# Unrolled middle batches, and softmax row shifts turned from columns to rows through DRAM

## The chip, the cores and the metric

One core of a Trainium2 chip runs the whole program. The metric is the device time of one execution in microseconds (us), as the median of the runs; the profile is of one further execution, and its own time is given beside it. The engines are named as in the profile: PE (matmul, with PEld for its weight loads), DVE (vector), ACT (scalar), POOL (GpSimd) and SP (the queue that issues nearly all DMAs).

## What is computed

A decoder layer on 16 batches of 256 tokens of width 128: a gated recurrence, cross-attention over 1601 context rows per batch with 16 heads of 64, and a mixture of 8 feed-forward experts, each followed by a layer norm. Nearly all of the time goes to the cross-attention:

```python
q = (x @ Wq + bq).reshape(b, lq, H, D)
k = (embeds @ Wk + bk).reshape(b, lk, H, D)
v = (embeds @ Wv + bv).reshape(b, lk, H, D)
scores = jnp.einsum('bqhd,bkhd->bhqk', q, k) * SCALE
attn = jax.nn.softmax(scores, axis=-1)
ctx = jnp.einsum('bhqk,bkhd->bqhd', attn, v).reshape(b, lq, AD)
return ctx @ Wo + bo
```

## The kernel before

The attention works through 16 batches times 8 pairs of heads. One pair of one batch is called a slot here; there are 128. Scores are made with the keys on the partitions and the 256 queries along the free axis, in 7 score units of up to two key tiles for both heads. So the softmax's row maximum, which is subtracted before the exponential, has to stand along the free axis too. It is found one slot ahead: for slot s + 1, PE makes the scores a second time with the queries on the partitions (`maximum`, L1304), DVE takes their maxima (`maxima`, L991), and `row_shift` on DVE reduces them to a negated column `nm` for each of the two query tiles (L998, first and second tile; the second comes after `keys_low` of chunk 0). The column is then widened to 128 equal columns (`nspread`, L1003), PE transposes both tiles (L1312) into a PSUM bank, and ACT copies the bank to `shift` (L742). The first of four matmuls of each score tile adds `shift` (L1330).

A slot runs in this order. PE: maxima of slot s + 1 and score units of slot s in turn; then values (L1293 to L1295) and keys (L1277 to L1279) of later slots, queries (L1284), in the second slot of a batch the output projection (L1360), the two transposes (L1312), in the sixth slot the transposes of the next batch's context (L1266), the denominators of slot s - 1 (L1351), and the product of slot s with the values (`attend`, L1342). ACT: `heads_out` (copy of the previous slot's product to `heads_raw`, L752), 14 exponentials (L763, L766), copies of values (L736), keys (L720) and queries (L725), `shift_out` (L742), in the sixth slot four copies of context (L716), and `sums_out` (copy of the denominators to `den`, L747). DVE: 16 maxima, `row_shift`, the low parts of keys and queries (L978, L984), in the sixth slot those of the context (L972), in the second `finish_rows`, and last `reciprocals` (L1009) and `normalise` (L1018), which makes `heads_T` from `heads_raw` and `rden`.

`heads_out` of a slot waits until the `normalise` of the slot before has read `heads_raw`:

```python
def heads_out(at, r):
    wait(act, norm_ok, at.n(1, r, 0))
    act.wait_ge(ring_full, at.full("pv", r))
    copy(heads_raw[:, :], ps[:, at.place_of("pv", r), 0:T]).then_inc(ring_act, 1)
```

The 8 PSUM banks go round as a ring in the order that `batch_fills` writes out: each product takes the bank that the product eight places before it has left. Of a slot's last products, `den` and `pv` hold the banks that score unit 1 of the next slot takes.

Each engine keeps its own order. The first and the last batch are written out (`batch(Batch("first", 0, B))` and so on); the 14 batches between are one body in a loop (`Fori`) on PE, ACT, DVE and POOL. SP has a loop of its own that loads the next batch's context once its place is read, and is otherwise idle during the attention. Every wait is a semaphore wait of the engine at the head of its queue: what stands behind it waits too.

## Time and profile before

| | us |
|---|---|
| median of 3 runs | 3018.2 |
| lowest and highest run | 3013.98 and 3557.24 |
| the profiled execution | 3013.75 |
| its span | 3011.9 |
| PE busy | 2779.7 (92%) |
| DVE busy | 2175.8 (72%) |
| POOL busy | 2125.0 (71%) |
| ACT busy | 1689.3 (56%) |

The span is the time from the first to the last instruction of the profiled execution. Rows of a timeline give the start in us from the start of the span, the duration in us, and then engine, source line, operation, the tiles written and read, and the count of merged instructions; what stands in brackets is idle time before the row and what ended it. A matmul's end is modelled; the distance between starts is the firmer number.

### The profile page before, as it was taken

The numbers are of one execution on the slowest core, as the hardware profiler recorded it, in microseconds if no ns is written. First come the engines' busy times: TensorE is split into PE (matmuls) and PEld (weight loads), VectorE is DVE, ScalarE is ACT, GpSimd is POOL, SyncE is SP. The second block draws the span as 40 slices with busy tenths as digits, with TensorE's granted clock in tenths as the row PEclk, the third lists the DMA queues.
The fourth block names the chain that finished last, engine by engine and source line by source line (L and its number), as shares of the span: only waits on it lengthen the run. The fifth ranks groups of instructions, "written<-read, shape, count | busy, mean of one in ns | idle before, by whom it ended". The sixth has DMA issues, their size and how long they took to land.

```text
span 3011.9 us, 80484 instructions
## 1 busy us (share of the span) xinstructions
PE 2779.7 (92%) x28504; PEld 2321.9 (77%) x28504; DVE 2175.8 (72%) x4113; ACT 1689.3 (56%) x3422; POOL 2125.0 (71%) x1708
## 2 busy tenths in 40 slices
PE   5799999999999999999999999999999999997371
PEld 3688888888888888888888888888888888886250
DVE  6777877877777778778777778778787777784104
ACT  2466665656656656656566666556566666663020
POOL 2377877777777777777777777777787777786305
PEclk8799999999999999999999999999999999998586
DMA  3100000000000000000000000000000000000032
GB/s 95 44 2 13 2 13 3 13 3 13 3 2 14 2 14 2 13 2 13 3 13 3 2 13 2 14 2 13 3 13 3 27 3 2 2 2 1 23 92 63
DMA packets 65430, 41.89 MB, mean 14 GB/s; under 512 B 6614, under 2 KB 62635, under 8 KB 65010
## 3 DMA queue, kind: packets, MB, share of 16 engines
q1 hardware_dynamic: 62962, 32.35, 3.8%
q8 instruction: 266, 4.36, 0.6%
q0 software_dynamic: 2048, 3.91, 0.5%
q14 instruction: 154, 1.26, 0.1%
HBM read 28.15 MB, written 8.39 MB: 12 GB/s over the span
## 4 chain that ended last, share of the span: by engine, by line
PE 89%; issue 5%; POOL 3%; DVE 1%; ACT 1%; DMA 0%; POOLq 0%; DVEq 0%; ACTq 0%
PE ps L1330 28%; PE ps L1342 24%; PE ps L1304 7%; PE ps L1293 4%; PE ps L1294 3%; PE ps L1295 3%; PE ps L1277 3%; PE ps L1278 3%; PE ps L1279 3%; PE ps L1351 2%; PE ps L1360 2%; PE ps L1284 2%; PE ps L1450 1%; PE ps L1457 1%; PE ps L1312 1%
## 5 line engine op out<-in xcount | busy, mean ns | idle before, releaser
L600 POOL TENSOR_TENSOR key_sums<-key_sums,prob_T 128x512 f32<-128x512 f32 (+1 forms) x1408 | 1812.3, 1287 | 124.3 <-ACT prob_T L763 8.1
L991 DVE TENSOR_REDUCE mx<-ps 128x1 f32<-128x400 f32 (+1 forms) x2048 | 1070.0, 570 | 476.4 <-PE ps L1304 438.9
L763 ACT ACTIVATE prob_T<-ps 128x512 f32<-128x512 f32 x1536 | 834.3, 596 | 222.0 <-PE ps L1330 203.3
L1342 PE MATMUL ps<-prob_T,v_sb 128*64 128x256 f32 (+1 forms) x6656 | 742.3, 380 | 0.8 <-ACT prob_T L766 0.8
L1342 PEld LDWEIGHTS ps<-prob_T,v_sb 128*64 128x64 f32 (+1 forms) x6656 | 478.4, 137 | 243.3 <-issue 2.1
L596 POOL TENSOR_TENSOR key_sums<-prob_T 128x512 f32<-128x512 f32 x128 | 165.1, 1290 | 509.8 <-ACT prob_T L763 509.8
L1330 PE MATMUL ps<-shift,shift_w 64*128 64x256 f32 (+1 forms) x3328 | 507.3, 300 | 0.3 <-DVE k_lo L978 0.2
L1330 PE MATMUL ps<-q_lo,k_hi 64*128 64x256 f32 (+1 forms) x3328 | 476.0, 279 | 1.8 <-issue 1.8
L1330 PE MATMUL ps<-q_hi,k_lo 64*128 64x256 f32 (+1 forms) x3328 | 474.1, 279 | 0.0
L1330 PE MATMUL ps<-q_hi,k_hi 64*128 64x256 f32 (+1 forms) x3328 | 473.0, 279 | 0.0
L752 ACT COPY heads_raw<-ps 128x256 f32<-128x256 f32 x128 | 47.7, 373 | 671.9 <-PE ps L1342 671.9
L1304 PE MATMUL ps<-k_hi,q_hi 64*128 64x400 f32 (+1 forms) x2048 | 371.2, 357 | 26.4 <-issue 23.4
L978 DVE SCALAR_TENSOR_TENSOR k_lo<-ps,bk_c,k_hi 128x400 fp32r<-128x400 f32 (+1 forms) x512 | 309.9, 625 | 57.1 <-ACT k_hi L720 51.9
L1330 PEld LDWEIGHTS ps<-shift,shift_w 64*128 64x128 f32 (+1 forms) x3328 | 310.2, 181 | 52.7 <-ACT prob_T L763 8.2
L1330 PEld LDWEIGHTS ps<-q_lo,k_hi 64*128 64x128 f32 (+1 forms) x3328 | 314.3, 183 | 3.2 <-issue 3.2
L1330 PEld LDWEIGHTS ps<-q_hi,k_lo 64*128 64x128 f32 (+1 forms) x3328 | 312.5, 182 | 0.0
L1330 PEld LDWEIGHTS ps<-q_hi,k_hi 64*128 64x128 f32 (+1 forms) x3328 | 312.4, 183 | 0.1
L720 ACT ACTIVATE k_hi<-ps,bk_c 128x400 fp32r<-128x400 f32 (+1 forms) x512 | 302.8, 596 | 13.1 <-PE ps L1279 9.8
L1304 PEld LDWEIGHTS ps<-k_hi,q_hi 64*128 64x128 f32 x2048 | 195.9, 186 | 77.6 <-issue 76.8
L736 ACT COPY v_sb<-ps 128x512 f32<-128x512 f32 x384 | 225.7, 588 | 52.9 <-PE ps L1295 25.8
L1293 PE MATMUL ps<-wv_hi,ctx_hi 128*128 128x256 f32 (+1 forms) x832 | 246.9, 297 | 0.0
L1009 DVE RECIPROCAL rden<-den 128x256 f32<-128x256 f32 x128 | 223.9, 1749 | 25.2 <-ACT den L747 24.8
(173 smaller groups left out, 3641.9 us busy)
## 6 DMA issues: line engine op xcount, KB each, us to landing
ctx_raw<-in_ctx_dram SPq DMA_DIRECT2D x16, 768.0 KB
tables<-in_L_ffn_W_dram SPq DMA_DIRECT2D x16, 256.0 KB, 3.9
slots_in<-zeros SPq DMA_DIRECT2D x32, 64.0 KB
xs<-in_x_dram SPq DMA_DIRECT2D x8, 256.0 KB, 3.2
xres<-in_x_dram SPq DMA_DIRECT2D x8, 256.0 KB, 2.9
v_sb<-slots_in SPq DMA_DIRECT2D x8, 256.0 KB, 2.8
slots_out<-v_sb SPq DMA_DIRECT2D x8, 256.0 KB, 4.1
out_dram<-x1s SPq DMA_DIRECT2D x8, 256.0 KB, 2.4
```

Source lines behind the costliest of these rows:

```text
L596: op = nc.gpsimd.tensor_tensor(acc[:, :, :], prob_T[:, :, 0, :], prob_T[:, :, 1, :], ALU.add)
L600: op = nc.gpsimd.tensor_tensor(acc[0:rows, :, :], acc[0:rows, :, :], prob_T[0:rows, :, k, :], ALU.add)
L720: nc.scalar.activation(k_hi[r % 2][:, KEY0[c]:KEY0[c] + WID[c]], ps[:, at.bank("k", r, c), 0:WID[c]], ACT.Identity, bias=bk_c[:, r % NJ:r ...
L736: copy(v_sb[:, g % 2, 2 * n:2 * n + 2, :], src).then_inc(ring_act, 1)
L763: nc.scalar.activation(prob_T[:, h, 2 * i:2 * i + 2, :].rearrange("p k t -> p (k t)"), ps[:, bank, :], ACT.Exp).then_inc(ring_act, 1)
L978: v.scalar_tensor_tensor(k_lo[r % 2][:, cols], ps[:, at.bank("k", r, c), 0:WID[c]], bk_c[:, r % NJ:r % NJ + 1], k_hi[r % 2][:, cols].bitca ...
L991: v.tensor_reduce(mx[:, qt, h, c:c + 1], ps[:, at.bank("mx", r, c, qt, h), 0:WID[c]], AX.X, ALU.max).then_inc(ring_dve, 1)
L1009: v.reciprocal(rden[:, :], den[:, :]).then_inc(rden_ok, 1)
L1293: mm(o, ctx_hi[:, cols], wv_hi[:, g0:g0 + 2 * P], start=True, stop=False)
L1304: mm(ps[:, banks[h], 0:WID[c]], q_hi[r % 2][lanes, qt * P:qt * P + P], k_hi[r % 2][lanes, KEY0[c]:KEY0[c] + WID[c]], start=True, stop=True ...
L1330: last = mm(ps[0:rows, banks[h], n * T:n * T + T], keys_part, query_part[lanes, :], start=(step == 0), stop=(step == 3))
L1342: last = mm(ps[h * DH:h * DH + DH, bank, 0:T], v_sb[0:rows, r % NJ // 2 % 2, k, v0 + h * DH:v0 + h * DH + DH], prob_T[0:rows, h, k, :], st ...
```

## The change

Two things are done at once. The 14 middle batches are written out on PE, ACT, DVE and POOL instead of looped over, and SP's instructions for them too. And the column `nm` is no longer widened and transposed by PE: SP stores it to DRAM, word by word, as rows, waits for that store, and reads it back twice, once for each head, each time as one 1 KB row broadcast to 64 partitions of a new tile `shift_f`; ACT rounds `shift_f` to `shift`. The bank `sh` of the ring, the copies L1003 and the transposes L1312 fall away.

```diff
@@ batch_fills
-        put("act", "sh", 0)
...
-        if following:
-            put("act", "sh", s + 1)
@@ decoder_layer
+    shift_dram = nc.dram_tensor("row_shifts", [2, 2 * QT, P], F32, kind="Internal").ap()
...
-        nm = sb("nm", [P, QT, 2])
-        nspread = sb("nspread", [P, QT, P])
+        nm = sb("nm", [P, 2, QT])
+        shift_f = sb("shift_f", [P, T])
@@ SP
+            def turn_shift(at, r):
+
+                sp.wait_ge(nm_ok, at.n(2, r, 2))
+                if at.kind != "start" and (at.kind != "first" or r > 1):
+
+                    sp.wait_ge(shift_in, at.n(32, r, -32))
+                with nc.allow_non_contiguous_dma(reason="a column of 128 values for each head and tile"):
+                    sp.dma_start(shift_dram[r % 2].rearrange("n p -> p n"), nm[:, :, :].rearrange("p h q -> p (h q)"))\
+                        .then_inc(shift_sent, 16)
+                sp.wait_ge(shift_sent, at.n(16, r, 16))
+                wait(sp, shift_ok, at.n(1, r, 0))
+                for h in range(2):
+                    sp.dma_start(shift_f[h * DH:h * DH + DH, :],
+                                 shift_dram[r % 2, h * QT:h * QT + QT, :].rearrange("q p -> (q p)")[None, :].broadcast_to([DH, T])).then_inc(shift_in, 16)
+
+            def batch(at):
+                for s in range(NJ):
+                    if s < NJ - 1 or at.kind != "last":
+                        turn_shift(at, s + 1)
+                    if s == 5 and at.kind != "last":
+                        next_context(at)
+
+            def next_context(at):
+
+                sp.wait_ge(ctx_hi_ok, at.b * 4 + 8)
+                load_context(at.b + 2)
+
             load_context(0)
-            with sp.Fori(1, B) as b:
-
-                sp.wait_ge(ctx_hi_ok, b * 4)
-                load_context(b)
+            sp.wait_ge(ctx_hi_ok, 4)
+            load_context(1)
+            turn_shift(Batch("start", 0, B), 0)
+            batch(Batch("first", 0, B))
+            for b in range(1, B - 2):
+                batch(Batch("mid", b, B))
...
@@ POOL; ACT, DVE and PE alike
-            with pool.Fori(1, B - 1) as b:
+            for b in range(1, B - 1):
                 batch(Batch("mid", b, B))
@@ ACT
             def shift_out(at, r):
-                act.wait_ge(ring_full, at.full("sh", r))
-                copy(shift[:, :], ps[:, at.bank("sh", r), 0:T]).then_inc(ring_act, 1)
+                act.wait_ge(shift_in, at.n(32, r, 32))
+                copy(shift[:, :], shift_f[:, :]).then_inc(shift_ok, 1)
@@ DVE
             def maxima(at, r, units):
+
+                wait(dve, nm_ok, at.n(2, r, 0))
...
-                v.tensor_reduce(nm[:, qt, :], mx[:, qt, :, :], AX.X, ALU.max, negate=True).then_inc(nm_ok, 1)
-                dve.wait_ge(nm_ok, at.n(2, r, qt + 1))
                 if qt == 0 and at.kind != "start" and (at.kind != "first" or r > 0):
 
-                    dve.wait_ge(ring_full, at.full("sh", r - 1))
-                v.tensor_copy(nspread[:, qt, :].rearrange("p (h d) -> p h d", h=2),
-                              nm[:, qt, :, None].broadcast_to([P, 2, DH])).then_inc(nspread_ok, 1)
+                    dve.wait_ge(shift_sent, at.n(16, r, 0))
+                v.tensor_reduce(nm[:, :, qt], mx[:, qt, :, :], AX.X, ALU.max, negate=True).then_inc(nm_ok, 1)
@@ PE
-            def row_shift(at, r):
-
-                pe.wait_ge(nspread_ok, at.n(2, r, 2))
-                bank = bank_of(at, "sh", r)
-                for qt in range(QT):
-                    last = tr(ps[:, bank, qt * P:qt * P + P], nspread[:, qt, :], ident[:, :])
-                last.then_inc(ring_full, 1)
-
             def score_unit(at, s, i):
...
-                                 also=[("k", s, 3), ("q", s), ("sh", s)] if i == 0 else [])
+                                 also=[("k", s, 3), ("q", s)] if i == 0 else [])
+                if i == 0:
+                    pe.wait_ge(shift_ok, at.n(1, s, 1))
```

## Rows read from the trace of the kernel before

**Rows 1.** The page: busy time and share of each engine
```profile
PE 2779.7 (92%) x28504; PEld 2321.9 (77%) x28504; DVE 2175.8 (72%) x4113; ACT 1689.3 (56%) x3422; POOL 2125.0 (71%) x1708
```
**Rows 2.** Windows cut at slots' first exponentials: from:to, length, busy time by engine, PEclk
```profile
300.37:2611.77 2311.40, 2286.10 (x24322) 1932.41 (x24321) 1790.30 (x3207) 1429.59 (x2912) 1767.97 (x1400) 1.00 0.03 7
2611.77:2632.20 20.43, 20.43 (x220) 17.09 (x218) 16.42 (x27) 13.00 (x26) 15.39 (x12) 1.00 0.01 2
2632.20:2655.15 22.95, 22.95 (x243) 19.62 (x241) 17.61 (x37) 12.25 (x26) 18.07 (x16) 1.00 0.01 1
...
199.54:218.92 19.38, 19.38 (x211) 16.00 (x209) 15.49 (x28) 12.13 (x26) 15.46 (x12) 1.00 0.01 2
239.29:260.04 20.75, 20.75 (x224) 17.47 (x222) 17.79 (x32) 13.62 (x30) 15.48 (x12) 1.00 0.15 41
179.16:199.54 20.38, 20.38 (x220) 17.05 (x218) 16.21 (x28) 13.01 (x27) 15.42 (x12) 1.00 0.01 2
```
**Rows 3.** Waits of PE: engine, line, releaser: total us, times, longest us
```profile
PE ps L1304 <- issue: 23.4, 13, 2.1
```
**Rows 4.** Timeline of PE, batch 0, third slot
```profile
191.51 0.38 PE L1312 MATMUL ps<-ident,nspread 128*128 128x128 f32 x2
191.82 0.65 PE L1351 MATMUL ps<-key_sums,ones 128*64 128x256 f32 x4
```
**Rows 5.** Groups by line: busy us, mean ns of one, idle before
```profile
L1003 DVE COPY nspread<-nm 128x128 f32<-128x128 f32 x256 | 222.9, 871 | 18.7
```
**Rows 6.** Timeline of ACT, batch 0, third slot and start of the fourth
```profile
192.13 0.37 ACT L742 CAST shift<-ps 128x256 fp32r<-128x256 f32 x1
192.58 0.37 ACT L747 COPY den<-ps 128x256 f32<-128x256 f32 x1
198.19 0.37 ACT L752 COPY heads_raw<-ps 128x256 f32<-128x256 f32 x1 [5.24 <-PE ps L1342]
199.54 1.71 ACT L763 ACTIVATE prob_T<-ps 128x512 f32<-128x512 f32 x3 [0.97 <-PE ps L1330]
```
**Rows 7.** Timeline of DVE, the same slot
```profile
192.98 1.75 DVE L1009 RECIPROCAL rden<-den 128x256 f32<-128x256 f32 x1
194.77 1.16 DVE L1018 TENSOR_TENSOR heads_T<-heads_raw,rden 128x256 f32<-128x256 f32 x1
```
**Rows 8.** The tile heads_T: durations in ns, shortest, median and longest
```profile
L1018 DVE TENSOR_TENSOR heads_T<-heads_raw,rden x128: 424/802/1505, 174.4 to 2777.4; 128x256 f32<-128x256 f32 x128
```
**Rows 9.** Timeline of DVE, batch 0, sixth slot
```profile
248.88 0.15 DVE L998 TENSOR_REDUCE nm<-mx 128x2 f32<-128x8 f32 x1
...
252.33 2.01 DVE L972 TENSOR_TENSOR ctx_lo<-ps,ctx_hi 128x512 fp32r<-128x512 f32 x4
```
**Rows 10.** Timeline of ACT, the same slot
```profile
251.27 0.37 ACT L742 CAST shift<-ps 128x256 fp32r<-128x256 f32 x1
251.52 1.70 ACT L716 CAST ctx_hi<-ps 128x512 fp32r<-128x512 f32 x4
```
**Rows 11.** Timeline of SP's queue, the same slot: start and duration of an issue
```profile
253.44 0.40 SPq L505 DMA_DIRECT2D ctx_raw<-in_ctx_dram  x1
254.06 0.52 SPq L507 DMA_DIRECT2D ctx_raw<-in_ctx_dram  x1
```
**Rows 12.** DMA issues: KB each, median us from issue to landing
```profile
slots_out<-v_sb SPq DMA_DIRECT2D x8, 256.0 KB, 4.1
...
w_rows<-in_L_attn_Wr_dram SPq DMA_DIRECT2D x1, 64.0 KB, 1.9
...
bo_b<-in_L_xattn_bo_dram SPq DMA_DIRECT2D x1, 64.0 KB, 2.7
decay_c<-in_L_attn_decay_dram SPq DMA_DIRECT2D x1, 0.5 KB, 2.1
...
bq_c<-in_L_xattn_bq_dram SPq DMA_DIRECT2D x1, 4.0 KB, 7.0
...
bv_c<-in_L_xattn_bv_dram SPq DMA_DIRECT2D x1, 4.0 KB, 3.4
```
**Rows 13.** Timeline of DVE, before the first slot
```profile
136.49 0.16 DVE L998 TENSOR_REDUCE nm<-mx 128x2 f32<-128x8 f32 x1
```
**Rows 14.** Timeline of PE, first score tile of the first slot
```profile
138.68 0.39 PE L1330 MATMUL ps<-shift,shift_w 64*128 64x256 f32 x2 [0.19 <-DVE k_lo L978]
```

More of the change, by code:

```diff
@@ L420, in decoder_layer @@
         nm_ok = sem("nm_ok")
-        nspread_ok = sem("nspread_ok")
+        shift_sent = sem("shift_sent")
+        shift_in = sem("shift_in")
+        shift_ok = sem("shift_ok")
         rden_ok = sem("rden_ok")
@@ L510, in load_context @@
                              C_IN[bass.ds(b * KEYS + KEYS - 1, 1)]).then_inc(ctx_in, 16)
-            load_context(0)
-            with sp.Fori(1, B) as b:
-                sp.wait_ge(ctx_hi_ok, b * 4)
-                load_context(b)
+            def turn_shift(at, r):
[19 more added lines that the diff above has]
+                load_context(at.b + 2)
+            load_context(0)
+            sp.wait_ge(ctx_hi_ok, 4)
[4 more added lines that the diff above has]
+                batch(Batch("mid", b, B))
+            at = Batch("mid", B - 2, B)
+            for s in range(NJ):
+                turn_shift(at, s + 1)
+            batch(Batch("last", B - 1, B))
             def load_weights(i, s):
@@ L807, in _ @@
             batch(Batch("first", 0, B))
-            with act.Fori(1, B - 1) as b:
+            for b in range(1, B - 1):
                 batch(Batch("mid", b, B))
@@ L1081, in _ @@
             batch(Batch("first", 0, B))
-            with dve.Fori(1, B - 1) as b:
+            for b in range(1, B - 1):
                 batch(Batch("mid", b, B))
@@ L1384, in batch @@
                         project(at)
-                    if following:
-                        row_shift(at, s + 1)
                     if s == 5 and more:
@@ L1407, in _ @@
             queries(at, 1)
-            row_shift(at, 0)
             batch(Batch("first", 0, B))
-            with pe.Fori(1, B - 1) as b:
+            for b in range(1, B - 1):
                 batch(Batch("mid", b, B))
```

## The prediction

> **What bounds the kernel now.** First the page's busy times [rows 1]: PE is busy for 92% of the span, DVE and POOL for 72% and 71%, ACT for 56%. An average hides stages, so next I cut the attention at the first exponential of each slot [rows 2]. The 14 looped batches take 2311.40 us, 165.1 each, with PE busy for 2286.10 of it; inside a slot PE has no idle time at all. So what comes off PE's queue shortens the slot, as long as nothing else becomes late. The waits of PE show where its 25 us of idle go: 13 times it stood still for 1.8 us on average (23.4 us in all), waiting for no one, ahead of the first maximum of a batch [rows 3]. Thirteen is the number of times that the loop goes back from the end of one of the 14 batches to the start of the next.
>
> **The loops.** Batch 0 and batch 15 are written out already, so they show what a written-out slot takes [rows 2]: 20.43 us for the first slot of a batch, 22.95 for the second, 20.38 for the third (the fifth and seventh do the same work, three in all), 19.38 for the fourth (the eighth does the same, two in all, with one value tile group fewer than the third), 20.75 for the sixth with the context. The sum is 20.43 + 22.95 + 3 x 20.38 + 2 x 19.38 + 20.75 = 164.03 us. Against 165.1 that is 1.07 us a batch, 15 us for 14. The stalls are worth 23 us, but the written-out slots are each a little slower than looped ones, or the difference would be larger. I take -15 (bounds 0, if new code stalls elsewhere, and -23).
>
> **PE's transposes.** Start to start, the two transposes take 191.82 - 191.51 = 0.31 us [rows 4], on the bounding engine, in each of 128 slots: -39.7 us. The matmul added in their place is none; a wait on `shift_ok` replaces one on the ring.
>
> **DVE's copies.** 256 copies of 871 ns, 222.9 us [rows 5], fall away. They cost nothing today: `row_shift` ends microseconds before PE needs it and DVE is idle each slot. I count 0. What they do is move the second `nm` forward. In the sixth slot the first copy happened to be short, and `nm` ended at 248.88 + 0.15 = 249.03, 9.74 us after the slot's start at 239.29 [rows 2, 9]. I use 9.74 for every slot after the change. ACT's copy stays, with SBUF instead of PSUM as its source, at 0.37.
>
> **The way through DRAM.** Call T the time from the end of the second `nm` to the start of ACT's copy. Its terms:
> - SP wakes: 0.2. ACT's last `ctx_hi` ends at 251.52 + 1.70 = 253.22 and SP issues at 253.44 [rows 10, 11].
> - The store, 128 partitions of 4 single words. No row shows a store of words. Nearest are loads of words [rows 12]: 128 words land after 2.1 us (`decay_c`), 1024 words after 3.4 (`bv_c`), and after 7.0 where 512 KB loads are ahead of them (`bq_c`). By interpolation 512 words take 2.1 + 384/896 x 1.3 = 2.7. Bounds 2.1 and 7.0. I take 2.7: with SP otherwise idle nothing is ahead, and the store of 65536 words in rows of 512 B lands after 4.1, so direction alone is not dear.
> - SP wakes again, 0.2, and issues the first load; the second follows 254.06 - 253.44 = 0.6 later [rows 11].
> - Each load is 64 KB. 64 KB land after 1.9 us (`w_rows`) or, as a broadcast row behind the bias loads, 2.7 (`bo_b`) [rows 12]. I take 2.0, and 0.1 for ACT to wake.
>
> T = 0.2 + 2.7 + 0.2 + 0.6 + 2.0 + 0.1 = 5.8 us; bounds 5.1 and 10.8.
>
> On the page "DMA: Bandwidth & Descriptors" (Anatomy of one DMA) the Trainium skill gives about 2.0 us fixed for each small transfer, most of it the receipt of the write. By it the store would take 2.0 and T would be 5.1, the low bound of the rows, which gives the 2962 us of the first rival below instead of 2977. The figure is fitted on GpSimd's path, and `decay_c` (2.1) agrees with it.
>
> **Who waits.** PE's next scores are not the first to suffer. ACT now waits for the loads at the head of its queue, and `sums_out` is behind it; DVE's reciprocal and `normalise` wait for `den`; and the next `heads_out` may not overwrite `heads_raw` before `normalise` is done. In the third slot, from the start of ACT's shift copy to the end of the reciprocal is 192.98 + 1.75 - 192.13 = 2.60 us [rows 6, 7], and `normalise` starts 0.04 later. It took 1.16 there, but 0.42 at its shortest [rows 8]; I take 0.42, as it would run after POOL's sums are done. Chain: 3.06 us.
>
> Its end may slip this far. The slot's successor starts at 199.54 - 0.31 = 199.23. `heads_raw` needs 0.37 before the exponential, and its bank is what score unit 1 waits for, about 0.1 before that; so it must start by 198.7, and `normalise` end by 198.65, 19.5 after the slot's start [rows 6]. ACT's copy must start by 19.5 - 3.06 = 16.4: T up to 6.7 is free in the four slots of this kind (first, third, fifth, seventh). The fourth and eighth are 1.00 us shorter [rows 2]: free up to 5.7. The sixth is 0.37 longer, but four context copies stand between shift and `den`. The low parts on DVE can start 0.8 after ACT's shift copy and take 2.01, then reciprocal and `normalise` add 2.2: 5.0 instead of 3.06 [rows 9, 10]. Free up to 19.87 - 5.0 - 9.74 = 5.1. In the second slot `finish_rows` keeps DVE busy and the slot is 2.5 us longer: free up to about 9. Past these limits each microsecond is a microsecond of the slot, because exponentials and score units then run in step with PE full. The score path itself would be late only 2 us later.
>
> Loss per batch: 4 x (T - 6.7) + 2 x (T - 5.7) + (T - 5.1), each if positive. At T = 5.8: 0.2 + 0.7 = 0.9, times 16 is +14 us. Once, before the first slot, nothing covers T: `nm` ends at 136.65, and the first score goes from 138.68 [rows 13, 14] to 136.65 + 5.8 + 0.37 + 0.1 = 142.9, +4 us.
>
> **The sum.** 3013.75 - 15 - 40 + 14 + 4 = 2977 us against the profiled execution. That one is 0.15% below the median of the runs (3018.2), and I forecast 2980.
>
> SP's queue: each slot adds three issues and four waits to it, and the context load now stands behind the turn of the seventh slot's shift. The load is needed 8 slots later, so this costs nothing.
>
> **Rivals.**
> - *All hidden.* T of 5.1 or less: the sum is 3013.75 - 55 + 3 = 2962. For it: `decay_c` at 2.1. Against it: 512 separate words, and `bo_b` at 2.7. Chance 0.25.
> - *The gain eaten.* T from 6.3 to 7.1, by `bo_b`'s 2.7 for the loads or a store of 3.5. At T = 6.55 the loss is 3 x 6.55 - 16.5 = 3.2 a batch, 51 us, and the time is that of before, 3014. Chance 0.21.
> - *The word store is slow.* Writing single words to DRAM takes over 4 us. From T = 7.2 the loss is 7 x 7.2 - 43.3 = 7.1 a batch, 114 us, and the kernel is over 2% slower. At T = 8 it is 12.7 a batch: 3013.75 - 55 + 203 + 6 = 3168. With `bq_c`'s 7.0 for the store T is 10.1 and the time about 3400. For it: no row shows a word store, and the slowest word load is 7.0. Against: that one stood behind large loads. Chance 0.15. The same page of the Trainium skill (Rules for kernel authors) says to transpose in the DMA hardware and never by a rearranged access pattern, a 19-fold difference, and that a transfer under 512 B is done as read-modify-write; no row here shows a store of that kind.
> - *Unrolling gives nothing.* New stalls for instructions in 14 written-out batches: 2995. Against it are the two batches already written out [rows 2]. It has 0.04 by itself.
>
> **Chances and range.** The likeliest, T from 5.1 to 6.3, has 0.35 (2962 to about 3000). I call over 2% faster or slower a difference, since a measurement of this kernel can't tell less from no change: the limits are 2958 and 3079. No case reaches 2958 by its terms; with removed stalls worth the full 23 us the best is 2954. So faster 0.07, slower 0.15, the rest 0.78. The range goes from 2955 to 3050 (T of 7), and leaves out the slow store.
>
> **What would show it.** The rows of `shift_f` among the DMA issues give the loads' landing, and the span from L998's second run to ACT's shift copy gives T. If T is under 5.1, a third slot is 20.07 us and a fourth 19.07; if it is over 6.7, ACT's idle time before `heads_raw` is put down to DVE's `heads_T`. PE's 13 waits for issue should be gone. The forecast is wrong if word stores are slow, if the slots' limits are not where I put them, or if the queue of instructions stalls PE elsewhere.

## The result, and the profile after

| | before | after |
|---|---|---|
| median, us | 3014.81 (6 runs) | 3924.2 (6 runs, 3922.25 to 3927.71) |
| the profiled execution's span | 3011.9 | 3924.5 |
| ratio to before | 1 | 1.3021 [1.3008, 1.3034] |

The changed kernel takes 30% longer; I had forecast 2980 us. One of the six runs of the kernel before took 3557.24 us, in a slower state of the chip, and the ratio leaves it out. The page of the profile already says what kind of loss it is. The first block is the page of the kernel after: span, busy time of each engine, the clock row in fortieths of the span, the shares of the chain that ended last, and the two DMA rows of the turn (KB each, median us from issue to landing; the store's row has no median).

```profile
span 3924.5 us, 71098 instructions
PE 3096.8 (79%) x28248; PEld 2576.5 (66%) x28248; DVE 1917.6 (49%) x3857; ACT 1682.4 (43%) x3422; POOL 2116.3 (54%) x1708
PEclk8788888888888888888888888888898988888766
DMA 39%; PE 34%; DVE 11%; ACT 7%; issue 6%; POOL 2%; SPq 1%; POOLq 0%; ACTq 0%; DVEq 0%
...
shift_f<-row_shifts SPq DMA_DIRECT2D x256, 64.0 KB, 3.4
row_shifts<-nm SPq DMA_DIRECT2D x128, 2.0 KB
```

Against [rows 1] PE does 256 matmuls fewer and yet is busy for 317 us more, and it is no longer the bound: its share fell from 92% to 79%, and no other engine rose in its place. DVE, ACT and POOL all have less or equal work in a longer span. The largest part of the chain is no engine at all but DMA. PE's extra busy time is the other half of the story: the clock row is nearly all eights, where it was nearly all nines before. The clock row of the kernel before, and the granted clock's mean in each kernel, before and after:

```profile
PEclk8799999999999999999999999999999999998586
core 0: 3011.9 us, clock 0.960
...
core 0: 3924.5 us, clock 0.856
```

The records show two levels only, 1.0 (2.4 GHz) and 0.5 (1.2 GHz), so 2 x (1 - 0.856) x 3924.5 = 1130 us of the span were at the lower one; summed over the stretches of the trace it is 1135 us, in 135 stretches, about one for each slot. In the kernel before it was 246 us, in 15 stretches.

Next, who waited. The waits of the kernel after (engine, line, released by: total us, times, longest us):

```profile
SPq L524 <- DMA row_shifts<-nm: 1038.8, 126, 10.3
ACT shift L775 <- DMA shift_f<-row_shifts: 1242.9, 128, 14.3
DVE rden L1041 <- ACT den L780: 1015.7, 113, 14.3
PE ps L1356 <- ACT shift L775: 352.5, 98, 12.5
ACT heads_raw L785 <- DVE heads_T L1050: 295.5, 126, 2.8
PE ps L1356 <- ACT heads_raw L785: 84.1, 111, 7.3
```

The lines are one chain. SP waits 8.2 us each time for its own store before it may issue the loads (L524). ACT stands at the head of its queue for the loads (L775), 9.7 us on average. Behind it stand `den` and so DVE's reciprocal (L1041), then `heads_T`, then `heads_raw` (L785), and PE's next scores wait for the shift itself in 98 slots and, one score unit later, for `heads_raw` in 111. PE is idle for 4.9 us of each slot in all. One slot of the kernel after in order of time. SP's queue:

```profile
1796.10 0.37 SPq L519 DMA_DIRECT2D row_shifts<-nm  x1
1804.34 1.08 SPq L524 DMA_DIRECT2D shift_f<-row_shifts  x2
```

ACT (what stands in brackets is the wait before the row):

```profile
1808.55 0.40 ACT L775 CAST shift<-shift_f 128x256 fp32r<-128x256 f32 x1 [10.14 <-DMA shift_f<-row_shifts]
1808.86 0.37 ACT L780 COPY den<-ps 128x256 f32<-128x256 f32 x1
1811.51 0.37 ACT L785 COPY heads_raw<-ps 128x256 f32<-128x256 f32 x1 [2.28 <-DVE heads_T L1050]
1811.77 0.60 ACT L796 ACTIVATE prob_T<-ps 128x512 f32<-128x512 f32 x1
```

DVE:

```profile
1795.91 0.15 DVE L1036 TENSOR_REDUCE nm<-mx 128x2 f32<-128x8 f32 x1
...
1809.26 1.75 DVE L1041 RECIPROCAL rden<-den 128x256 f32<-128x256 f32 x1 [10.15 <-ACT den L780]
1811.05 0.42 DVE L1050 TENSOR_TENSOR heads_T<-heads_raw,rden 128x256 f32<-128x256 f32 x1
```

The slot starts at 1785.07 (its first exponential) and the next one at 1811.77. `nm` is done at 1796.06, 10.99 after the start; SP has issued the store 0.04 later; then 8.24 us pass until SP may issue a load; ACT's copy starts at 1808.55, so T is 12.49; and from there the next slot's first exponential is 3.22 away. 10.99 + 12.49 + 3.22 = 26.70, the whole slot. Compare the third slot of before at 20.38 [rows 2], in which the copy and the reciprocal had nearly the same lengths (0.37 and 1.75) and `heads_T` a longer one (1.16) [rows 6, 7], and all of it lay under PE's work.

What PE does meanwhile is in the windows of the same slot of after, cut where its last scores are formed (1793.50) and once more among its products (1799.60); columns as in [rows 2]:

```profile
1785.07:1793.50 8.43, 8.28 (x103) 7.72 (x104) 6.88 (x15) 6.59 (x14) 5.93 (x5) 0.84 0.01 2
1793.50:1799.60 6.10, 6.10 (x47) 5.14 (x47) 3.98 (x10) 4.54 (x10) 5.62 (x5) 1.00 0.05 3
1799.60:1811.77 12.17, 7.22 (x62) 4.90 (x58) 2.48 (x3) 0.94 (x3) 3.81 (x3) 0.85 0.07 11
```

And PE's own rows, the last three of one slot's scores and then the first ones of the next:

```profile
1792.52 0.28 PE L1356 MATMUL ps<-q_hi,k_hi 64*65 64x256 f32 x2
1792.63 0.28 PE L1356 MATMUL ps<-q_lo,k_hi 64*65 64x256 f32 x2
1792.75 0.28 PE L1356 MATMUL ps<-q_hi,k_lo 64*65 64x256 f32 x2
...
1809.10 0.58 PE L1356 MATMUL ps<-shift,shift_w 64*128 64x256 f32 x2 [4.68 <-ACT shift L775]
1809.45 0.45 PE L1356 MATMUL ps<-q_hi,k_hi 64*128 64x256 f32 x2
1809.66 0.45 PE L1356 MATMUL ps<-q_lo,k_hi 64*128 64x256 f32 x2
1809.87 0.45 PE L1356 MATMUL ps<-q_hi,k_lo 64*128 64x256 f32 x2
```

PE stands still for 4.68 us, and behind the gap nearly the same matmuls start 0.21 us apart that started 0.11 to 0.12 apart before it: the clock is at its lower level. The trace's clock record has it fall at 1808.18, inside the gap, and rise again at 1815.00, 3.2 us into the next slot, whose first stretch forms the scores. The slot shown began in the same way (0.84 in its first window). A score matmul with the shift as its operand takes 365 ns on average against 300 before. `nm` itself moves with it: its mean end is 11.39 us into the slot, not at the 9.74 that I had assumed from [rows 9].

### The profile page after: what moved, and what is told of

Same layout as the page of the kernel before. It is cut to its first block, busy times and chain, and to the rows that moved or that the text cites. A ratio compares the mean times of both kernels' runs of the same rounds, so it can differ in the third digit from the quotient of the medians.

```text
span 3924.5 us, 71098 instructions
## 1 busy us (share of the span) xinstructions
PE 3096.8 (79%) x28248; PEld 2576.5 (66%) x28248; DVE 1917.6 (49%) x3857; ACT 1682.4 (43%) x3422; POOL 2116.3 (54%) x1708
## 4 chain that ended last, share of the span: by engine, by line
DMA 39%; PE 34%; DVE 11%; ACT 7%; issue 6%; POOL 2%; SPq 1%; POOLq 0%; ACTq 0%; DVEq 0%
DMA row_shifts<-nm 28%; PE ps L1356 24%; DMA shift_f<-row_shifts 11%; DVE rden L1041 6%; PE ps L1336 5%; DVE k_lo L1011 2%; ACT v_sb L769 2%; ACT k_hi L753 2%; PE ps L1325 1%; SPq L524 1%; DVE heads_T L1050 1%; ACT heads_raw L785 1%; ACT den L780 1%; PE ps L1327 1%; PE ps L1326 1%
## 5 line engine op out<-in xcount | busy, mean ns | idle before, releaser
L1356 PE MATMUL ps<-shift,shift_w 64*128 64x256 f32 (+1 forms) x3328 | 621.6, 365 | 514.2 <-ACT shift L775 352.5
L1356 PEld LDWEIGHTS ps<-shift,shift_w 64*128 64x128 f32 (+1 forms) x3328 | 407.9, 236 | 627.0 <-issue 375.5
L1041 DVE RECIPROCAL rden<-den 128x256 f32<-128x256 f32 x128 | 224.2, 1752 | 1015.7 <-ACT den L780 1015.7
L775 ACT CAST shift<-shift_f 128x256 fp32r<-128x256 f32 x128 | 51.7, 404 | 1242.9 <-DMA shift_f<-row_shifts 1242.9
L1356 PE MATMUL ps<-q_hi,k_hi 64*128 64x256 f32 (+1 forms) x3328 | 567.9, 331 | 0.0
L1356 PE MATMUL ps<-q_lo,k_hi 64*128 64x256 f32 (+1 forms) x3328 | 564.9, 329 | 0.0
L1356 PE MATMUL ps<-q_hi,k_lo 64*128 64x256 f32 (+1 forms) x3328 | 561.6, 327 | 0.0
L1336 PE MATMUL ps<-k_hi,q_hi 64*128 64x400 f32 (+1 forms) x2048 | 426.4, 407 | 116.1 <-ACT heads_raw L785 113.4
L1356 PEld LDWEIGHTS ps<-q_hi,k_hi 64*128 64x128 f32 (+1 forms) x3328 | 414.5, 240 | 0.5
L1356 PEld LDWEIGHTS ps<-q_lo,k_hi 64*128 64x128 f32 (+1 forms) x3328 | 411.8, 238 | 0.0
L1356 PEld LDWEIGHTS ps<-q_hi,k_lo 64*128 64x128 f32 (+1 forms) x3328 | 408.5, 236 | 0.0
```

Source lines behind the costliest of these rows:

```text
L1041: v.reciprocal(rden[:, :], den[:, :]).then_inc(rden_ok, 1)
L1336: mm(ps[:, banks[h], 0:WID[c]], q_hi[r % 2][lanes, qt * P:qt * P + P], k_hi[r % 2][lanes, KEY0[c]:KEY0[c] + WID[c]], start=True, stop=True ...
L1356: last = mm(ps[0:rows, banks[h], n * T:n * T + T], keys_part, query_part[lanes, :], start=(step == 0), stop=(step == 3))
```

## The experiments

In the tables below T is, as in the prediction, the mean time from the end of the second `nm` to the start of ACT's copy to `shift`.

### The loops alone

The kernel before, with its middle batches written out on PE, ACT, DVE and POOL; the transposes stay.

```diff
-            with pe.Fori(1, B - 1) as b:
+            for b in range(1, B - 1):
                 batch(Batch("mid", b, B))
```

> The kernel before with only its 14 middle batches written out; shifts still turned by TensorE. If the 13 stalls of 1.8 us at the loop's seams go and each written-out slot is as long as those of batches 0 and 15, the time is 15 us under before, ratio 0.995. If written-out code stalls elsewhere, the ratio is 1.000 or more. If the unrolling had a share in the 30% of the whole change, it is over 1.02.

Measured: 3010.89 us, ratio 0.9986 [0.9977, 0.9995]. So the loops are no part of the loss. Writing them out gained 4.3 us of the 15 forecast. The waits of this kernel name where a part went:

```profile
PE ps L1304 <- ACT heads_raw L752: 10.2, 14, 0.7
```

The 13 stalls for issue are gone; instead PE waits 14 times, 0.7 us each, for ACT to read `heads_raw` before the first maximum of a batch. Middle batches take 165.0 us, with the eighth slot at 20.16 us, where I had put 19.38 for it from the fourth; the other slots are within 0.05 of the written-out ones in [rows 2]. The reason for the eighth lies in the ring's numbering and is tried below.

### The way through DRAM alone

The kernel after with the four loops put back (SP's stays written out).

```diff
-            for b in range(1, B - 1):
+            with pe.Fori(1, B - 1) as b:
                 batch(Batch("mid", b, B))
```

> The changed kernel with the loops of the 14 middle batches put back on PE, ACT, DVE and POOL; SP stays written out. If the way through DRAM alone is the loss, the time is that of the changed kernel plus at most 25 us for the seams, 3925 to 3950 us, with the same 12.5 us from the last column to ACT's copy. If the unrolling has a share in the loss, it is well under 3900.

Measured: 4027.01 us, ratio 1.3366 [1.3345, 1.3387]. T is 13.16 and a slot 28.5 us. The whole loss is here, and more than the 3950 that I had put as the most: the loops cost 103 us beside the new wait, where they cost 4 without it. The store and the loads landed later by 0.5 and 0.1 us than in the kernel after. Why loops on four other engines should delay a store is not settled; only the sum is.

### Taking `den` out of the queue behind the shift

The chain from ACT's copy over `den` to `heads_raw` exists only because `sums_out` stands behind `shift_out` in ACT's queue. Here it stands ahead.

```diff
-                    if following:
-                        shift_out(at, s + 1)
                     if s == 5 and more:
                         for c in range(4):
                             context_high(at, NJ, at.b + 1, c)
                     if before:
                         sums_out(at, s - 1)
+                    if following:
+                        shift_out(at, s + 1)
```

> The changed kernel with one order altered on ACT: the denominators' copy (and the context copies of the sixth slot) stand ahead of the copy that waits for the loads. If a slot is as long as it is because sums_out, reciprocal and normalise queue behind the wait, they leave the chain: 2.6 to 3.1 us less a slot, but the first score unit then waits for the shift itself, 22.9 + 0.4 + 1.3 = 24.6 us a slot instead of 27.7, and the time is about 3925 - 128 x 3 = 3540 us. If only the lateness of the shift matters and the chain behind it is hidden, the time stays at 3925.

Measured: 3815.17 us, ratio 1.2658 [1.2639, 1.2678]. A miss in size: 109 us came back, not 384. The chain did leave, as this kernel's waits show:

```profile
ACT shift L775 <- DMA shift_f<-row_shifts: 1203.2, 128, 14.7
PE ps L1356 <- ACT shift L775: 492.2, 113, 12.5
...
DVE rden L1041 <- ACT den L780: 30.8, 2, 21.1
```

DVE's 1015.7 us of waiting for `den` fell to 30.8 and `heads_raw` waits no longer for `heads_T`, but PE's wait for the shift went from 352.5 to 492.2. The slot is only 0.9 us shorter (26.79). `nm` is done 0.5 us earlier (10.85) and from ACT's copy to the next exponential it takes 2.7 us instead of 3.8, since there are still scores to form behind the shift; but T itself grew by 0.76 to 13.26, because the store landed later (9.20 us on average instead of 8.67). Why it did isn't settled. The order in ACT's queue is a small part; the late shift is the large one.

### What each form of store costs

The loops-alone kernel with one extra DMA in each slot, issued by SP at the moment when `nm` is ready. SP waits for it, and nothing else does but DVE's write of `nm` a slot later, by when it has long landed. The eight slots of a batch take eight forms, so each form runs 15 or 16 times. In the slots of the changed form the two broadcast loads follow it.

```diff
+    pr = [nc.dram_tensor(f"probe{n}", shape, F32, kind="Internal").ap() for n, shape in enumerate((
+        [4, P], [P, 4], [P, 4, 16], [P, 4, P], [2, P], [4, P, 16], [4, P]))]
...
+                    if form == 0:
+                        d = sp.dma_start(pr[0].rearrange("n p -> p n"), src)
+                    elif form == 1:
+                        d = sp.dma_start(pr[1], src)
+                    elif form == 2:
+                        d = sp.dma_start(pr[2][:, :, 0], src)
```

> Shifts turned by TensorE as before, middle batches written out, and beside it, waited for by nobody but SP, one DMA form per slot of a batch, 16 times each: slot 0 the changed kernel's store of 512 words as 4 rows (and its two loads), 1 a store of 128 runs of 16 B, 2 a store of 512 words each into a 64 B place of its own, 3 the same with 512 B places, 4 a store of 256 words as rows, 5 a store of 512 pieces of 64 B as rows, 6 four loads of one column of 128 words each from SBUF into a row in SBUF, 7 a load of 512 words from DRAM. If the store's 8.7 us come from several DMA engines writing words of the same 64 B, forms 2, 3 and 5 land within 3 us and form 0 takes 8.7. If any write of a word to DRAM is slow, forms 2 and 3 take 8.7 too and 5 is fast. If the number of 512 descriptors is what costs, form 5 and 7 take about 8.7 too, and form 4 about half. If it is contention with the attention's own traffic, form 0 is faster or slower here than 8.7 by as much as that.

Measured: 3011.25 us in a single run, as the kernel it is built on. From issue to last landing, median us of each form, from the trace's record of the DMAs' semaphore:

```
512 words as 4 rows (the changed form)      9.32  (8.48 to 10.83)
256 words as 2 rows                         8.43
512 words, each in 64 bytes of its own      2.38
512 words, each in 512 bytes of its own     2.07
512 pieces of 64 bytes, as rows             1.76
128 runs of 16 bytes (row of 4 a partition) 1.41
4 columns of 128 words, SBUF to an SBUF row 2.0 each, issues 0.6 apart
load of the same 512 words                  2.13
the two broadcast loads                     3.2
```

Two rows of SP's queue of this kernel show it without the semaphore's record:

```profile
1465.54 0.39 SPq L529 DMA_DIRECT2D probe<-nm  x1
1474.04 1.14 SPq L554 DMA_DIRECT2D xres<-probe  x2
```

SP issues the store at 1465.54, waits for it, and can issue the loads at 1474.04, 8.50 us later, in a kernel in which PE runs at full speed and nobody waits for this store. So the wait isn't made by the slowed kernel around it. Nor is it the number of words: the same 512 words, one every 64 bytes, land in 2.38 us, and half of them packed side by side still take 8.43. Nor is it their reading or sending, as far as the packets' record goes: the last packet of the changed form is over 1.3 us after the issue. What is late is the semaphore's last step, behind all packets.

### How many words may share 64 bytes

The same kernel with other forms: 512 words as 4 rows, with 8, 4, 2 and 1 of them in each 64 bytes; 4 words of one partition in one place; one column of 128 words alone.

```diff
-        [4, P], [P, 4], [P, 4, 16], [P, 4, P], [2, P], [4, P, 16], [4, P]))]
+        [4, P, 2], [4, P, 4], [4, P, 8], [4, P, 16], [P, 4, 4], [1, P], [4, P]))]
...
+                    if form < 4:
+                        d = sp.dma_start(pr[form].rearrange("n p x -> p n x")[:, :, 0], src)
```

> The probe kernel with other stores to DRAM, one a slot, waited for by SP alone: slots 0 to 3 the 512 words as four rows with 8, 4, 2 and 1 words in each 64 B; slot 4 the four words of a partition 16 B apart in one 64 B place; slot 5 one column of 128 words side by side; slots 6 and 7 the changed kernel's form. If writes to one 64 B place go one after the other, time follows their number: 16 words 9.3, 8 words about 5.5, 4 about 3.6, 2 about 2.6, 1 about 2.2, slot 4 about 3.6, and one column of 128 words as slow as 256 were, 8 or more. If the total of words side by side is what counts, slot 5 lands in half the time of 256 words, about 4.

Measured (a single run, 3011.32 us), the same record:

```
words in each 64 bytes        16     8     4     2     1
512 words as 4 rows, us     8.94  3.96  2.58  1.90  1.87
4 words of one partition in 64 bytes        3.46
one column of 128 words side by side        7.40
```

The time falls as the words move apart and is flat from two words a place on. (The form of the changed kernel took 9.32 us in the first slot of a batch and 8.94 and 8.88 in the seventh and eighth, so the place in the batch is worth some 0.4 us.) The number of words hardly matters (128 take 7.40, 512 take 8.94), the number that share a place of 64 bytes does: (8.94 - 1.87) / 15 = 0.47 us for each word beyond the first. The steps are not even, though (0.30 us a word from 1 to 8, 0.62 from 8 to 16), and four words of one partition (3.46) cost more than four from different ones (2.58), so a plain queue of equal writes is not the whole of it. Nor is sharing a place dear by itself: the runs of 16 bytes of the kernel above share each 64 bytes between four partitions too, and land after 1.41 us. And 64 bytes is only the unit in which I count: as 32 bytes between words are no dearer than 64, the runs show that close packing of single words costs, and not at what boundary. All three middle forms and the single column came in under what I had expected.

### The changed kernel with the store spread out

This is the same test in the place that counts: the kernel after, its store going to places 64 bytes apart.

```diff
-                    sp.dma_start(shift_dram[r % 2].rearrange("n p -> p n"), nm[:, :, :].rearrange("p h q -> p (h q)"))\
+                    sp.dma_start(shift_far[r % 2].rearrange("n p x -> p n x")[:, :, 0], nm[:, :, :].rearrange("p h q -> p (h q)"))\
```

> The changed kernel with one thing altered: the store of 512 words goes to places 64 B apart, in a tensor of its own. The two loads read the old place, which holds zeros, so the shifts are left out of the output (the exponentials are not shifted); every wait and transfer stays. If the writes into shared 64 B places are what makes the changed kernel slow, the store lands after 1.9 us instead of 8.7, T falls from 12.5 to 5.7, and the time is between 2990 and 3030. If the loads or the chain of waits have a large share of their own, it is over 3200.

Measured: 3002.9 us, ratio 0.9954 [0.9937, 0.997]. One changed address pattern takes away 921 us, all of the 909 us lost and 12 more. T is 5.40. The two loads still read the old place, which holds zeros, so this kernel leaves the shifts out of its output. The waits of this kernel, and its DMA rows:

```profile
ACT shift L780 <- DMA shift_f<-row_shifts: 331.5, 128, 6.1
...
ACT heads_raw L790 <- DVE heads_T L1055: 142.1, 55, 3.0
```

```profile
shift_f<-row_shifts SPq DMA_DIRECT2D x256, 64.0 KB, 2.6
row_shifts_far<-nm SPq DMA_DIRECT2D x128, 2.0 KB, 1.9
```

The store lands after 1.9 us instead of 8.5, in the same number of packets. `heads_raw` still waits for `heads_T` in 55 slots, and the slots are 20.31, 22.55, 20.25, 19.24, 20.28, 20.55, 20.27 and 20.56 us on average. So at T of 5.4 the kernel is near what I had forecast for 5.8, and above it by 26 us, of which the dearer loops are 11 and the cheaper transposes 13. The loads here landed after 2.6 us, against 3.4 in the kernel after. They read rows written once, long before; whether it is that, or the idle neighbourhood, that makes them faster wasn't told apart. Of the 7.1 us by which T fell the store has 6.6 and the loads have 0.5. No run reads the spread words back, so what a load of words 64 bytes apart costs is not shown, and neither is a correct kernel with a spread store.

### The turn without DRAM

The column can reach its place without a round trip: four copies from a column in SBUF to a row in SBUF, one for each head and tile, on rows 0 and 64 of `shift_f`, with a weight of 1 for those two rows and 0 for the others.

```diff
...
+                    for h in range(2):
+                        for q in range(2):
+                            sp.dma_start(shift_f[h * DH:h * DH + 1, q * P:q * P + P].rearrange("o (p a) -> o p a", a=1),
+                                         nm[:, h, q:q + 1]).then_inc(shift_in, 16)
...
-            v.memset(shift_w[:, :].bitcast(F32), SPREAD)
+            own(v.memset(shift_w[:, :].bitcast(F32), 0.0))
+            own(v.memset(shift_f[:, :], 0.0))
+            for h in range(2):
+                v.memset(shift_w[h * DH:h * DH + 1, :].bitcast(F32), 1.0)
```

> The changed kernel with the way through DRAM replaced: SP copies each of the four columns of 128 words straight into a row of SBUF (two rows on partition 0, two on partition 64 of shift_f, zeros elsewhere), and the score matmul adds row 0 and row 64 through a weight of 1 there instead of the mean over 64 equal rows; shapes and counts of matmuls are unchanged. From the probe a column lands 1.65 us after its issue and issues are 0.65 us apart: 0.03 + 3 x 0.65 + 1.65 = 3.6 us from the last nm to ACT's copy. If slots are limited as the prediction put it, all of it is hidden and the two transposes come off PE: 3011 - 128 x 0.31 = 2971 us, ratio 0.985. If DMAs in flight or ACT's wait cost by themselves, it is above 3000.

Measured: 2984.37 us, ratio 0.9908 [0.9891, 0.9924]. T is 4.05. SP's queue and the waits of this kernel:

```profile
1498.24 2.40 SPq L518 DMA_DIRECT2D shift_f<-nm  x4
```

```profile
ACT shift L769 <- DMA shift_f<-nm: 157.2, 128, 4.6
...
PE ps L1333 <- ACT heads_raw L779: 9.7, 14, 1.0
```

T is 0.4 us over what I had expected, since I took 1.65 for a column's landing; from its issue to its landing a column took 2.0 in the kernel with the eight forms, and 2.0 to 2.1 here. The four issues take 2.40 us of SP's time, the last of them starts 1.8 to 1.9 us after the first, and with its landing that is all of T. ACT waits 1.2 us a slot, and nobody behind it. The gain against the loops-alone kernel is 3010.89 - 2984.37 = 26.5 us; I had expected 40. From the start of the queries to the start of the denominators' matmul PE takes 0.74 us with the two transposes between them and 0.53 without (11.82 to 12.56 into the slot before, 11.94 to 12.47 here). So the transposes are worth 0.21 us each slot, and 128 x 0.21 = 27, which leaves nothing for DVE's removed copies.

### Where T starts to cost

The kernel above with small stores, each waited for, ahead of its four copies: three of them, then six. Nothing reads what they write.

```diff
+                for i in range(3):
+                    sp.dma_start(idle_dram[:, :], nm[:, :, :].rearrange("p h q -> p (h q)")).then_inc(shift_sent, 16)
+                    sp.wait_ge(shift_sent, at.n(48, r, 16 * i + 16))
```

> e5_sbuf_row with three small stores of 128 runs of 16 B, each waited for, ahead of the four copies: a delay of 3 x 1.45 and nothing else. T is about 7.9 us. By the prediction's limits the loss is 7 x 7.9 - 43.3 = 12 us a batch, 192 in all, and the time about 2971 + 192 = 3163. If the limits lie lower, because the half clock after a wait of PE costs on top, it is over 3200; if they lie higher it is under 3100.

> The same with six such stores: T is about 12.3 us, as late as in the changed kernel (12.5), with no transposing store and no broadcast load. If lateness alone makes the 30%, a slot takes 27.5 us and the time is 3880 to 3930. If traffic of the transposing store hinders others, it is clearly less. The prediction's line alone would give 7 x 12.3 - 43.3 = 42.8 a batch, 3656.

| | T | `nm` done | slot, mean | half clock | us | ratio |
|---|---|---|---|---|---|---|
| no store | 4.05 | 9.75 | 20.38 | 227 | 2984.37 | 0.9908 [0.9891, 0.9924] |
| three | 9.98 | 11.04 | 24.84 | 745 | 3551.12 | 1.178 [1.176, 1.1799] |
| six | 15.9 | 11.06 | 30.75 | 1489 | 4315.62 | 1.4339 [1.4297, 1.438] |

Both times were above what I had expected, since each small store, taken at 1.45 us, cost 2 us with its issue and the wait. By the T that they did get they test the price (half clock is the time at 1.2 GHz in us, `nm` done the mean time from the slot's start). From three to six T grows by 5.9 us and the kernel by (4315.62 - 3551.12) / 128 = 5.97 us a slot: past its limit each microsecond of T is a microsecond of the slot, with no DRAM word in it that shares a place. And at three stores the forecast's own line, with the second slot past its limit too ("about 9" in the forecast, 9.2 by the same sum), gives 4 x (9.98 - 6.7) + 2 x (9.98 - 5.7) + (9.98 - 5.1) + (9.98 - 9.2) = 27.3 a batch, 437 us, and the later `nm` adds (11.04 - 9.75) x 128 = 165: 602 together, against 567 measured over the kernel without a store. At six it gives 74.7 a batch, 1195, and 168 for `nm`: 1363, against 1331.

As to whether lateness alone makes the 30%: on the straight line between these two kernels a T of 12.5 gives 3877 us, 892 over the kernel without a store, and the kernel after has 940. That is an interpolation, but it leaves under 50 us for anything that the store to DRAM does besides being late.

### The ring numbered on across batches

This is about the extra wait of the written-out batches, and it gives the fastest kernel of these runs. The ring's banks were numbered anew in each batch, back from its end; a middle batch has 329 fills here (337 in the kernel before), one more than a multiple of eight. So the first maximum of a batch takes the very bank that the last product of the batch before still holds. Written-out batches don't need to be alike, so here the numbering runs on.

```diff
-def bank_at(kind, place):
+def origin(kind, b):
...
-    return RING[(place - len(FILLS[kind])) % len(RING)]
+    n = {k: len(f) for k, f in FILLS.items()}
+    return {"start": 0, "first": n["start"], "end": n["start"] + n["first"] + (b - 2) * n["mid"] + n["last"]}.get(
+        kind, n["start"] + n["first"] + (b - 1) * n["mid"])
...
-        return bank_at(self.kind, PLACE[self.kind][key])
+        return RING[(origin(self.kind, self.b) + PLACE[self.kind][key]) % len(RING)]
...
```

> e5_sbuf_row with the ring of PSUM banks carried on over the batches' seams. A middle batch has 337 - 8 = 329 products (8 x 41 + 1), so with banks counted back from a batch's end its first maximum takes the very bank that the last product of the batch before still holds, and waits for ACT's heads_raw. In e1_loops and e5_sbuf_row the eighth slot is 0.7 to 0.8 us longer than the fourth, which does the same work. If that bank is the cause, the eighth slot becomes as long as the fourth, 15 x 0.75 = 11 us less: 2973 us, ratio 0.987. If something else at the seam holds PE, nothing changes: 2984, ratio 0.991.

Measured: 2973.13 us, ratio 0.9858 [0.9841, 0.9874]. It gains 11 us on the kernel without the renumbering (0.9908 [0.9891, 0.9924]), PE no longer waits for `heads_raw` at a maximum, and the eighth slot went from 19.88 to 19.14 us, the length of the fourth. That settles the cause of the eighth slot: 14 x 0.74 = 10.4 us.

## Why the prediction was wrong

**The step that failed** is the second term of T, the store's 2.7 us. The store took 8.66. Each term beside what the kernel after shows, without the turn before the first slot (T of 13.88 there):

| term of T | taken | bounds | measured |
|---|---|---|---|
| SP wakes | 0.2 | | 0.03 |
| store, issue to last landing | 2.7 | 2.1 to 7.0 | 8.66 mean (7.44 to 10.43) |
| SP wakes again | 0.2 | | 0.02 |
| second load's issue | 0.6 | | 0.49 |
| load and ACT's wake | 2.1 | | 3.3 |
| T | 5.8 | 5.1 to 10.8 | 12.50 (11.99 to 13.55) |

The store accounts for 6.0 of the 6.7 us. I had interpolated it from loads of words [rows 12], by the number of words. The load of the very same 512 words lands after 2.13 us, so as a price of a load the 2.7 was fair. But a load of words writes to SBUF and only reads DRAM; no row of before showed words written to DRAM, and I named the gap ("no row shows a word store") and still put even its upper bound from loads. I said that the store of `slots_out` shows that "direction alone is not dear"; it is in rows of 512 bytes, and pieces of 64 bytes are indeed as cheap (1.76). What is dear is single words packed closely in DRAM. The bound of 7.0, the slowest word load, was also too low: 8.66. And the 2.0 us that the prediction set beside the rows as another price of the store is short of it by 6.7.

My rule was that what no row shows is bounded by the nearest rows. Here the nearest rows were near in size and in count and far in the one thing that counts, which end of the transfer is cut into words. A store whose rows in DRAM are made of words from 128 partitions deserved no upper bound taken from loads, and a chance well over 0.15. The Trainium skill warned of this pattern on the page "DMA: Bandwidth & Descriptors", which I quoted in the rival: don't transpose by a rearranged access pattern (Rules for kernel authors), and below 512 B a transfer is a read-modify-write (Specifications, and not the section that the rival names). The direction of the first agrees with the 8.66 us here; its factor of 19 is against a transpose in the DMA hardware, which no run here has. An explanation by small size alone does not agree: 512 words of 4 bytes each in their own 64 bytes are as small and landed after 1.9 to 2.4 us.

**The rival that came true** is the slow word store. Its condition, that single words written to DRAM take over 4 us, is narrower in the runs: it holds for packed words only. The links behind it were right as far as the waits show them. Its highest figure, about 3400 us for T of 10.1, is short of 3924 for two reasons, T of 12.5 and a cost that stood nowhere in my working.

**The cost that I left out** is the clock. PE is idle for 4.9 us of a slot in the kernel after, and the granted clock falls to 1.2 GHz about once a slot, in 94 of 126 cases inside one of PE's gaps of over 0.5 us. It comes back 3.7 us into the next slot (median), among its scores: 1135 us at the lower level against 246. `nm` waits for that phase. Over the first fifteen batches it is done at 11.39 instead of the 9.76 of the kernel with T of 4.05, so the loss was 1.63 us more each slot than any line in T could say. Not all of that is shown to be the clock's: after the slot's first exponential PE also waits 0.6 us a slot for `heads_raw`. In the kernel with `den` ahead of the shift that wait is gone, the lower clock is not, and `nm` is done at 10.85, 1.1 us later than in the kernel with T of 4.05. How the other 0.5 us divide is open, and no run holds the clock apart from the gaps. With both put in, the line comes near: 7 x 12.5 - 43.3 = 44.2 a batch, 707 us; the second slot past its limit of 9.2, 3.3 x 16 = 53; the later `nm`, 1.63 x 128 = 209; the first slot 11. 3013.75 - 4 - 27 + 707 + 53 + 209 + 11 = 3963, against 3924 measured. The 39 us between them, 0.3 a slot, are not assigned.

**The chain of who waits** held, though it is the smaller part: with `den` taken out of it, 109 of the 909 us came back. ACT's queue passes the lateness on to `den`, `rden`, `heads_T` and `heads_raw`, as told; from the copy's start to the end of `heads_T` it takes 1811.47 - 1808.55 = 2.92 us in the slot shown, where I had 3.06. The slope past the limits is 1 between the kernels with three and six small stores. The limits themselves may have been a little generous: the kernel with the spread store, at T of 5.40 (4.91 to 7.14), is 18.5 us above the one with 4.05 (about 14 by their ratios to the kernel before), where the line gives 16 x 0.3 = 5 at the mean. Single late turns account for some of that; how much was not worked out.

**PE's transposes** are worth 0.21 us a slot, not 0.31: -27 instead of -40. I took the distance between two starts in [rows 4], from the first transpose to the denominators' matmul. From the start of the queries to the transposes it is 0.43 us in the kernel before, and without the transposes it is 0.53 from the queries to the denominators' matmul: what stands behind the queries starts 0.10 later than the transposes did, and the rest of the 0.31 is the gain. The distance that would have given it is from the instruction before the removed ones to the one behind them, less the same distance without them; the second of these no row of before has.

**The loops** gave -4, not -15. The sum of slots from [rows 2] was sound but for the eighth, which I took to be like the fourth. In a written-out middle batch the boundary between batches comes with it, and there the ring's numbering makes PE wait (20.16 us instead of 19.38, 0.78 x 14 = 11 us: the whole difference). Batch 0's eighth slot, written out in the kernel before, had it already: it goes from 280.41 to 300.37, 19.96 us, and ends on this row of the kernel before, which I had not looked for:

```profile
298.90 0.45 PE L1304 MATMUL ps<-k_hi,q_hi 64*128 64x400 f32 x2 [0.55 <-ACT heads_raw L752]
```

**DVE's copies** were rightly counted at nothing: the 26.5 us gained by the turn without DRAM are the transposes'. **SP's queue** was too: in the kernel after no engine waits for the context load during the attention.

## What to carry to other kernels

A column from SBUF can be turned to a row by DMA at little cost if the destination is SBUF. Single words from 128 partitions, packed side by side in DRAM, took 7 to 11 us until they had landed; spread apart they took 1.9 to 2.4, but their way back was not tried. Put a round trip on the path only after its duration is measured in that very form and direction: a load of the same words tells nothing of the store. And when a wait is put on a path whose slack is used up, its price isn't only the wait: here TensorE's pauses also came with its lower clock, and the next phase ran slower too.

## What the runs showed of the hardware

- A store of single words to DRAM lands the later the closer they are packed: with 16, 8, 4, 2 and 1 of them in each 64 bytes 512 words took 8.94, 3.96, 2.58, 1.90 and 1.87 us. The packets are over after 1.3 us in the slowest form; the semaphore's last step comes 7 to 8 us behind them.
- Runs of 16 bytes, one from each partition, landed after 1.41 us, also where four of them share 64 bytes of DRAM; a column of 128 words to a row in SBUF after 2.0.
- A broadcast of one 1 KB row of DRAM to 64 partitions took 3.4 us here and 2.6 where the row had been written long before, against 1.9 for 64 KB of distinct rows [rows 12].
- SP goes on 0.02 to 0.03 us after the semaphore that it waits for, and its issues are 0.5 to 0.65 us apart.
- TensorE, idle for 4.9 us in each slot of 27.7, had the clock at 1.2 GHz for 29% of the span; idle for 2.9 us in each slot of 24.8 (three small stores), for 21%.
